# The beginnings of the attention passes: the first tile's power in two halves, its transposes behind its projections, and a first slot with an order of its own

## What is computed

```
h = shift_token(x)                       # half of the channels from the row before
q, k, v = split(h @ wqkv)                # 8 heads of 64
q = l2norm(q) * q_scale                  # divided by the norm over the 64 of a head
k = l2norm(k) * k_scale
q, k = rotary_xpos(q, k)                 # x * cos + rotate_half(x) * sin, scaled
o = local_attention(q, k, v)             # 128 queries against their own and the previous 128 keys
x = x + o @ wo
```

## Time and profile before

| what | us |
|---|---|
| median of 3 runs | 3055.84 |
| lowest, highest | 3054.52, 3057.24 |
| the profiled execution | 3054.01 |
| its span in the trace | 3052.2 |
| PE busy in the span | 2911.6 (95%) |
| DVE, ACT, POOL busy | 2364.6, 1745.7, 1695.9 |

### The profile page before, as it was taken

The page is one execution under the profiler, slowest core; times in us unless marked ns, Lnnn a source line. Parts: engine busy times, 40 slices in busy tenths (PEclk is TensorE's granted clock), DMA queues, the critical chain, the costliest instruction groups (busy, mean ns, idle before and its releaser), DMA issues.

```text
span 3052.2 us, 95332 instructions
## 1 busy us (share of the span) xinstructions
PE 2911.6 (95%) x34226; PEld 2544.8 (83%) x34226; DVE 2364.6 (77%) x6541; ACT 1745.7 (57%) x4596; POOL 1695.9 (56%) x1852
## 2 busy tenths in 40 slices
PE   6999989989998999999999989989999899999889
PEld 4888878878887888887788878878888788888778
DVE  6888777677777787777777777767777788887777
ACT  4777742267777224775777762247777422554445
POOL 7778830078887223333888851048888344437621
PEclk9999999999999999999999999999999999999999
DMA  4121121012211101000121121111211200100001
GB/s 142 44 73 41 44 81 38 24 35 63 47 41 41 44 21 43 11 11 22 38 69 41 42 62 52 30 30 43 68 42 43 64 21 7 28 1 1 1 15 41
DMA packets 178761, 122.64 MB, mean 40 GB/s; under 512 B 27532, under 2 KB 175336, under 8 KB 178024
## 3 DMA queue, kind: packets, MB, share of 16 engines
q1 hardware_dynamic: 177432, 117.77, 14.3%
q10 hardware_dynamic: 1104, 1.90, 0.2%
HBM read 48.29 MB, written 20.98 MB: 23 GB/s over the span
## 4 chain that ended last, share of the span: by engine, by line
PE 81%; DVE 7%; issue 4%; POOL 3%; SPq 2%; ACT 1%; DMA 1%; DVEq 0%; POOLq 0%; ACTq 0%
PE bank L376 7%; PE bank L378 7%; PE bank L377 7%; PE pair_bank L560 6%; PE scores L521 5%; PE scores L376 4%; PE scores L377 4%; PE scores L378 4%; PE bank L491 3%; PE pair_bank L782 2%; PE pair_bank L781 2%; PE pair_bank L780 2%; PE pair_bank L376 2%; PE scores L730 2%; PE scores L731 2%
## 5 line engine op out<-in xcount | busy, mean ns | idle before, releaser
L2722 POOL TENSOR_TENSOR prob<-prob,rsum 128x384 f32<-128x384 f32 x512 | 457.5, 922 | 253.0 <-DVE rsum L1919 253.0
L1255 ACT ACTIVATE prob<-prob,nmax 128x192 f32<-128x192 f32 x1024 | 451.9, 443 | 158.7 <-DVE nmax L1913 158.7
L1457 ACT ACTIVATE gate<-scores,bias 128x512 f32<-128x512 f32 x192 | 132.4, 689 | 511.2 <-PE scores L378 511.2
L2709 POOL TENSOR_TENSOR rn<-ss,mhalf 128x16 f32<-128x16 f32 x128 | 375.3, 2932 | 10.7
L376 PE MATMUL bank<-wqkv_hi,hT_hi 128*128 128x512 f32 x768 | 334.5, 436 | 8.3 <-DVE hT_lo L1852 4.0
L2716 POOL TENSOR_TENSOR qk<-rot_t 128x512 f32<-128x512 f32 x256 | 322.6, 1280 | 21.0 <-DVE ss L1886 14.3
L1913 DVE CUSTOM_DVE_ANT_0 prob<-scores,masks,rn 128x192 f32<-128x192 f32 x768 | 267.4, 414 | 65.9 <-PE scores L521 65.5
L2690 POOL TENSOR_TENSOR rstd<-meanvar,eps 128x4 f32<-128x4 f32 x48 | 11.2, 234 | 552.4 <-DVE meanvar L1844 552.4
L378 PE MATMUL bank<-wqkv_hi,hT_lo 128*128 128x512 f32 x768 | 304.6, 397 | 0.0
L377 PE MATMUL bank<-wqkv_lo,hT_hi 128*128 128x512 f32 x768 | 302.7, 394 | 0.0
L1924 DVE TENSOR_TENSOR OT_lo<-pair_bank,OT_hi 128x512 fp32r<-128x512 f32 x128 | 88.5, 692 | 185.5 <-ACT OT_hi L1271 185.5
(11 more groups left out here) (340 smaller groups left out, 9551.6 us busy)
## 6 DMA issues: line engine op xcount, KB each, us to landing
Vlo<-V SPq DMA_DIRECT2D x256, 64.0 KB, 2.0
Vhi<-V SPq DMA_DIRECT2D x256, 64.0 KB, 2.0
H<-Y SPq DMA_DIRECT2D x128, 64.0 KB, 1.8
H<-ya SPq DMA_DIRECT2D x128, 64.0 KB, 1.9
yb<-Y SPq DMA_DIRECT2D x128, 64.0 KB, 1.6
HB<-Y SPq DMA_DIRECT2D x32, 256.0 KB, 2.8
HB<-yb SPq DMA_DIRECT2D x32, 256.0 KB, 3.1
raw<-in_L_ffn_wqkv SPq DMA_DIRECT2D x4, 1536.0 KB
```

The source lines that it names most:

```text
L1255: e.activation(pb, pb, ACT.Exp, bias=nm[r][:, x:x + 1], scale=-1.0, accum_out=sums[r][:, x:x + 1]).then_inc(s_acEX[gi], 1)
L2709: e.tensor_tensor(rn[u][:, :], ss[u % 2][:, :], mhalf[:, :], ALU.pow).then_inc(s_plRN, 1)
L2722: e.tensor_tensor(pair, pair, rs[:, 2 * gi:2 * gi + 2].unsqueeze(2).to_broadcast([P, 2, KW]), ALU.mult).then_inc(s_plPN[gi], 1)
```

## The change

It touches `begin()` and slot 0 of runs 0, 1 and 3, on all four computing engines.

- POOL: the power of tile 0 is made in two halves of 8 columns by `first_pow`, k's behind k's addition and with a semaphore of its own (`s_plRK`), q's behind q's addition. `wo_weights` and the first mask come behind both, in all three runs. k's addition of tile 1 moves from slot 0 into `begin()`, ahead of q's. `first_slot()` on POOL has the four `pn_` of tile 0 first and then q's addition and the power of tile 2.
- DVE: `norm_(0)` stands right behind the rotary products of q of tile 0 and waits for `s_plRK` only; `sc_` of tile 0 waits for q's power. The k rotary of tile 1 and the low part of `ht(2)` come behind it and ahead of `ln_stats(1)` and `finish`. The rotary and sum of q of tile 2 move from `begin()` into `first_slot()`.
- PE: both groups of transposes of tile 0 stand behind `ht(2)`, ahead of the q projection of tile 1 (which now waits for ACT's copy of `bank[0]`, `qT_read(0)`). The q projection of tile 2 moves from `begin()` into `first_slot()`, behind q's transposes of tile 1 and ahead of v of tile 2. The wait for the last feed-forward rows (`s_dvYB`) moves to the end of `begin()`.
- ACT: the same order. k's squares of tile 2 move from slot 0 into `begin()`, and in `first_slot()` q's copy of tile 1 and `ht(3)` stand between the first four and the last four exponentials.

The list of all semaphores, which also gets the new one, is left out of the diff.

```diff
--- before.py
+++ after.py
@@ -328,7 +328,7 @@
         g_peKV, g_dvKV, g_acK, g_peKK, g_dvC, g_peQ = sem("g_peKV"), sem("g_dvKV"), sem("g_acK"), sem("g_peKK"), sem("g_dvC"), sem("g_peQ")
         g_acQ, g_peO, g_dvS2, g_dvA2, g_acO, g_plR2 = sem("g_acQ"), sem("g_peO"), sem("g_dvS2"), sem("g_dvA2"), sem("g_acO"), sem("g_plR2")
         g_peU, g_acXN, g_plO, g_dvU = sem("g_peU"), sem("g_acXN"), sem("g_plO"), sem("g_dvU")
-        g_plBO, s_plXB = sem("g_plBO"), sem("s_plXB")
+        g_plBO, s_plXB, s_plRK = sem("g_plBO"), sem("s_plXB"), sem("s_plRK")
         everything = [s_prepV, *s_x, s_raw, s_lndvST, s_lndvAG, s_lnplRV, s_lndvXN, s_lnsST, s_prepA, s_prepB, s_small, s_raw2,
                       *s_ld, s_prepP, s_stb, *s_vs, *s_st,
                       s_peHT, s_acHT, s_dvHT, s_peV, s_acV, s_plRN, *s_peQK, *s_acSQ, *s_dvRT, *s_dvSS, *s_plAD, s_dvQN, *s_peKT,
...
@@ -446,12 +446,16 @@
                     G = R0 + T
                     early = isinstance(T, int) and T < 3
                     e.wait_ge(s_dvHT, G + 1 + OFF)
-                    if j == 0 and not early:
+                    if j == 0 and isinstance(T, int) and T == 3 and run != DEPTH:
+                        q_read(2)
+                    elif j == 0 and not early:
                         qT_read(T - 2)
-                    elif j == 0 and T == (1 if run == DEPTH else 2):
+                    elif j == 0 and run == DEPTH and T == 1:
                         qT_read(0)
+                    elif j == 0 and run == DEPTH and T == 2:
+                        q_read(1)
                     elif j == 0 and T > 0:
-                        q_read(T - 1)
+                        qT_read(T - 1)
                     elif j == 1 and (not early or spare(run, T)):
                         k_read(T - 1)
                     proj(bank[j], u, INNER * j, INNER).then_inc(s_peQK[j], 1)
@@ -476,6 +480,8 @@
                     e.wait_ge(s_plAD[0] if j == 0 else s_dvQN, G + 1 + OFF)
                     if j == 0 and isinstance(T, int) and T == 0 and run == DEPTH:
                         v_read(0)
+                    elif j == 0 and isinstance(T, int) and T < 2 and run != DEPTH:
+                        q_read(T)
                     elif j == 0 and inside(T + 1):
                         q_read(T + 1)
                     elif j == 0:
@@ -619,15 +625,28 @@
                     qk_(1, 1, 1)
                     v_(0, 0)
                     ht(2, 2)
+                    tr_(0, 0, 1)
+                    tr_(0, 0, 0)
+                    qk_(1, 1, 0)
+                    qk_(2, 2, 1)
+                    v_(1, 1)
                     e.wait_ge(s_prepB, need['B'] + 4 + OFF)
                     if run:
                         e.wait_ge(s_dvYB, U * GRP * run + OFF)
-                    qk_(1, 1, 0)
-                    tr_(0, 0, 1)
-                    qk_(2, 2, 1)
-                    v_(1, 1)
-                    tr_(0, 0, 0)
+
+                def first_slot():
+                    sc_(0, 0)
+                    ht(3, 3)
+                    tr_(1, 1, 0)
                     qk_(2, 2, 0)
+                    v_(2, 2)
+                    pt_(0, 0, 0)
+                    pt_(0, 0, 1)
+                    tr_(1, 1, 1)
+                    qk_(3, 3, 0)
+                    pt_(0, 0, 2)
+                    pt_(0, 0, 3)
+                    qk_(3, 3, 1)
 
                 def begin_in_linear():
                     last = NT - 1
@@ -666,7 +685,10 @@
                 else:
                     begin()
                 for u in range(U):
-                    slot(u, u)
+                    if u == 0 and run != DEPTH:
+                        first_slot()
+                    else:
+                        slot(u, u)
                     if u < 2:
                         e.wait_ge(s_prepB, need['B'] + 4 + u + OFF)
                 with e.Fori(0, NIT - 2) as i:
@@ -1315,11 +1337,25 @@
                     qk_(1, 1, 1)
                     v_(0, 0)
                     ht(2, 2)
+                    tr_(0, 0, 1)
+                    tr_(0, 0, 0)
                     qk_(1, 1, 0)
-                    tr_(0, 0, 1)
+                    qk_(2, 2, 1)
                     v_(1, 1)
-                    tr_(0, 0, 0)
+
+                def first_slot():
+                    sc_(0, 0, 0)
+                    tr_(1, 1, 0)
+                    ht(3, 3)
+                    sc_(0, 0, 1)
                     qk_(2, 2, 0)
+                    v_(2, 2)
+                    pt_(0, 0, 0)
+                    pt_(0, 0, 1)
+                    tr_(1, 1, 1)
+                    qk_(3, 3, 0)
+                    pt_(0, 0, 2)
+                    pt_(0, 0, 3)
 
                 def begin_in_linear():
                     last = NT - 1
@@ -1349,9 +1385,11 @@
                     begin_in_linear()
                 else:
                     begin()
-                slot(0, 0)
                 if run == DEPTH:
+                    slot(0, 0)
                     linear_tail['yn'](NT - 1)
+                else:
+                    first_slot()
                 for u in range(1, U):
                     slot(u, u)
                 with e.Fori(0, NIT - 2) as i:
@@ -1887,7 +1925,10 @@
 
                 def norm_(T, u, j):
                     G = R0 + T
-                    e.wait_ge(s_plRN, 2 * G + 2 + OFF)
+                    if isinstance(T, int) and T == 0 and run != DEPTH:
+                        e.wait_ge(s_plRK, 2 * (run if run < DEPTH else run - 1) + 2 + OFF)
+                    else:
+                        e.wait_ge(s_plRN, 2 * G + 2 + OFF)
                     e.wait_ge(s_plAD[j], G + 1 + OFF)
                     e.tensor_tensor(heads(half(u, j)), heads(half(u, j)), rn[u][:, j * HEADS:(j + 1) * HEADS].unsqueeze(2).to_broadcast([P, HEADS, DH]), ALU.mult).then_inc(s_dvQN, 1)
 
@@ -1895,6 +1936,9 @@
                     G = R0 + T
                     r = u % 2
                     m = mask0 if u == 0 else mask1
+                    if isinstance(T, int) and T == 0:
+                        e.wait_ge(s_plRN, 2 * G + 2 + OFF)
+                        e.sem_inc(s_passed, 1)
                     if u == 0:
                         e.wait_ge(s_plM0, GRP * run + T // U + 1 + OFF)
                         e.sem_inc(s_passed, 1)
@@ -1969,22 +2013,33 @@
                     sum_(0, 0, 1)
                     sum_(0, 0, 0)
                     qk_(0, 0, 0)
+                    norm_(0, 0, 1)
+                    qk_(1, 1, 1)
+                    ht(2, 2)
                     if run == 0:
                         ln_stats(1)
                     if finish:
                         finish()
-                    qk_(1, 1, 1)
-                    ht(2, 2)
-                    norm_(0, 0, 1)
                     sum_(1, 1, 1)
+                    qk_(1, 1, 0)
                     sum_(1, 1, 0)
-                    qk_(1, 1, 0)
                     if run == 0:
                         ln_norm(1)
                         ln_stats(2)
                         e.wait_ge(s_raw2, need['raw2'] + OFF)
+
+                def first_slot():
+                    sc_(0, 0)
+                    rs_(0, 0, 0)
+                    norm_(1, 1, 1)
+                    qk_(2, 2, 1)
+                    rs_(0, 0, 1)
                     qk_(2, 2, 0)
+                    ht(3, 3)
+                    sum_(2, 2, 1)
                     sum_(2, 2, 0)
+                    qk_(3, 3, 0)
+                    sum_(3, 3, 0)
 
                 def begin_in_linear():
                     last = NT - 1
@@ -2030,7 +2085,12 @@
                     begin()
                 if run:
                     e.wait_ge(s_stb, 16 * GRP * ((run + 1) // 2) + OFF)
-                iteration(0)
+                for u in range(U):
+                    if u == 0 and run != DEPTH:
+                        first_slot()
+                    else:
+                        slot(u, u)
+                    extra(0, u)
                 with e.Fori(0, NIT - 2 if run else GRP - 4) as i:
                     iteration(i + 1)
                 if run == 0:
@@ -2666,7 +2726,6 @@
                     e.wait_ge(s_peW2, U * GRP * run + OFF)
                     e.memset(kT[:, :, U - 1, :], 0.0).then_inc(s_prepB, 1)
                     e.memset(V[U - 1][:, :], 0.0).then_inc(s_prepB, 1)
-                    wo_weights()
 
             def v_weights():
                 raw3 = raw[:, :].rearrange('p (k n) -> p k n', k=KD)
@@ -2735,8 +2794,15 @@
                         mask_of(it + 1)
                     if run == 0 and u == U - 1 and not (isinstance(it, int) and it > GRP - 4):
                         ln_rstd(it + 3)
-                if run:
+                if run == DEPTH:
                     mask_of(0)
+
+                def first_pow(j, done, before):
+                    w = slice(j * HEADS, (j + 1) * HEADS)
+                    e.wait_ge(s_dvSS[j], R0 + 1 + OFF)
+                    e.tensor_scalar(ss[0][:, w], ss[0][:, w], 1e-24, None, ALU.max).then_inc(done, 1)
```

(21 more changed lines are left out.)

2 lines of the change are left out of this document (1 added, 1 removed).

## The result

The changed kernel takes 3064.53 us (median of 14 runs, 3060.31 to 3067.76), the one before 3057.34 on the same chip (14 runs, 3053.58 to 3064.53). The ratio is 1.0024, 95% interval 1.0016 to 1.0031: slower by 7.2 us, or 0.24%, just beyond the 0.2% that the forecast counted as no change. The forecast was 3055.4 with a range of 3049 to 3060.5, "no change" with 0.83. The profiled run took 3065.52 us, 11.5 more than the profiled run of before (3054.01), which was one of the quickest of its kernel.

What follows compares the result with a forecast made beforehand. PE, 81% of the chain that ended last, was taken as the bound, so only its gaps could pay. +2.4 (run 0) - 2.2 (run 1) - 0.6 (run 3) = -0.4 us: 3053.6 profiled, 3055.4 median, range 3049 to 3060.5.

Steps and rivals of the forecast that it cites:

- Part 1: POOL and DVE, beginnings of runs 1 and 3: half power 1.65 us; norm delayed by q's addition, 1.24 us sooner.
- Part 2: PE's new order in the beginnings of runs 1 and 3: scores of tile 0 start 1.3 us sooner.
- Part 3: Slot 0 of runs 1 and 3: 2.0 us gap on q's copy, slot 12.7 us long, 0.7 more than before.
- Part 4: Run 0: tile 0's scores at 38.4 instead of 39.06, but the layer norm chain makes it lose 2.4 us.
- run 0's slot: Slot 0 of run 0: near 15.7 us long, scores of tile 1 at 54.1 instead of 51.68.
- the clock's term: Run 1, slot 0: 2.2 us sooner if PE keeps its clock, 0.6 if not; 2.2 was taken.
- half chance of one slow beginning: Lower clock staying in one beginning of runs 0, 1 and 3: the sum becomes +0.4 instead of -0.4 us.
- Rival B: Run 0's POOL queue delays tile 1's power and first `pn_`, PE's clock falls: +6.1 us, 3062; chance 0.07.
- worse norm: Slot 0, DVE's norm of tile 1 behind a second `pn_`: 0.9 us in each of runs 1 and 3.
- Rival A: Gaps of all three beginnings close as they look, nothing blocks the norm: 9.4 us gained, 3046.4; chance 0.10.

Runs made afterwards that it cites:

- e1: The changed kernel plus unused matmuls filling PE's two new gaps in runs 0, 1 and 3; ratio 1.0011 to the kernel before.
- e11: The change in runs 1 and 3 alone, each of the two gaps filled by two plain float32 matmuls; ratio 0.9988 to the kernel before.
- e12: The change in run 0 alone, layer norm statistics ahead of k's norm, gaps filled by 8 and 17 matmuls; ratio 1.0006 to the kernel before.
- e8: The kernel before with only POOL's power in halves, k's norm waiting for k's half, in runs 0, 1 and 3; ratio 0.9992.

## Why the prediction was wrong

**Right, to 0.2 us in runs 1 and 3: the order of events at full clock.** Part 1: a half takes 1.67 us (forecast 1.65). The norm met q's addition and took 1.74 us, and it ended 0.54 behind the addition. Part 2: 1.3 us sooner at the scores of tile 0; measured at full clock 17.41 against 18.70. Part 3: slot 0 of 12.7 us; measured 12.5 (e1, e11), with the gap on ACT's `qT` (2.13 against 2.0) and no wait for POOL at the first `pt_`. Part 4: scores of tile 0 in run 0 0.66 us sooner; measured 0.64 (e12) and 0.63 (e1). The first `pn_` stands behind `ln_rstd(2)`.

**Too small: run 0's slot.** The forecast had a slot of 15.7 us and 2.4 lost. That e12 measures 15.76 and 2.5 is no proof of it, since e12 has the statistics moved. With them where the change puts them it is 16.7 and 3.5, an estimate from e1 (above). The term that was too small is `ln_norm(1)`, 3.13 us in the sum and 4.11 in e1, in the chain that ends last there.

**Wrong: the clock's term.** The forecast took -0.4 us, and in it is -1.6 for the clock: run 1 was to be 2.2 sooner "if PE keeps its clock, 0.6 if not". The half chance of one slow beginning (+0.4 in all) was named and not taken. Measured, the way from the full-clock places to those of the changed kernel is 38.79 - 35.8 = 3.0 us in run 0, 33.88 - 29.90 = 3.98 in run 1 and 33.74 - 29.89 = 3.85 in run 3. That is 10.8 us, less the 1.6 that before's run 1 had: +9.2 where the forecast had -1.6. With run 0's 3.5 and the orders' gains of 0.8 in each of runs 1 and 3 it makes 9.2 + 3.5 - 1.6 = 11.1, the 11.0 us that the beginnings lost.

The step that failed is in part 2: PE "has lost one projection (1.4) from `begin()`, and its gaps have stayed: 2.4 us ahead of k's transposes", against 0.6 + 1.56 before. The 0.6, which the earlier trace rows leave out, is this:

```profile
621.79 0.47 PE L376 MATMUL bank<-wqkv_hi,hT_hi 128*128 128x512 f32 x1 [0.59 <-issue]
```

The forecast booked this as no change, since the sum of the idle time was nearly the same (3.3 against 3.0 us). The clock doesn't go by the sum: behind 1.54 to 2.22 us at this place it never fell, behind 2.46 to 2.60 always. Of the slot's gap the rows had shown one fall in three; that was taken for chance, and 1.6 us for the price of any fall. But in a changed beginning the clock falls twice, and what follows at half speed is projections, the longest work there.

The rule of the Trainium skill that the prediction quoted ("TensorE: Matmul & The Clock Gate", "HAM oscillation": idle gaps bring the clock down and what follows runs slow) was the right one, and the trace after agrees (0.43 us a matmul behind both gaps, 0.23 elsewhere). The section warns of longer gaps than the 2.46 us that were enough here; the measurement decides. The prediction set the rule aside because the earlier trace rows showed it once in three.

Rival B had the clock in it for run 0, but took the POOL queue for its cause and 0.07 for its chance; its 3062 lies nearer to 3064.5 than the forecast. That is luck in part. `ln_rstd(1)` did wait 1.64 us longer, but the first `pn_` then waited 1.33 us for DVE, so GpSimd's queue did not end last, and the "worse norm" did not come; B's clock terms (1.6 in run 0, 1.6 still in run 1) were too small. Rival A is refuted: a norm that meets nothing is had only by leaving it where it was (e8, 0.68 us), not by moving it forward.

Part 1's own fault was smaller. The split was costed only together with the norm's new place. Left in its old place, the norm gains 0.9 us by the split, against 1.3 at tile 0 in the new order, and TensorE's gaps become shorter instead of longer.
